# A graph attention layer in 128 rounds: how empty rows are found, who does additions and low parts, the order of scores and values, and how turned weights are loaded

## The chip, the core and the metric

One core of a Trainium2 chip. The metric is the time of one execution on the device in microseconds, as the median of several runs.

## The reference

x is (128 graphs, 128 nodes, 512), adj is (128, 128, 128). Per graph, with 16 heads of 32:

```python
q, k, v = heads(x @ Wq.T), heads(x @ Wk.T), heads(x @ Wv.T)
a = einsum('bhnd,bhmd->bhnm', q, k) * D ** -0.5 + (adj + adj)[:, None]
a = where(any(a != 0, axis=-1, keepdims=True), a, -inf)   # a row of zeros only is empty
p = nan_to_zero(softmax(a))
o = merge(einsum('bhnm,bhmd->bhnd', p, v)) @ Wo.T
return layernorm(x + o)                                   # eps 1e-5, no scale or shift
```

## The kernel before, in words

Four graphs form a group, and four heads a tile, so there are 32 groups of 4 rounds ("phases", PHASES = 128): round f treats group f // 4 and heads 4 (f % 4) to 4 (f % 4) + 3 of its four graphs. Each engine has an order of work written out by hand, and semaphores join the orders.

Precision: the weight products take operands split in a high part (rounded to FP32R) and a low part (the rest), and each product is 12 matmuls of 512 columns: low times high, high times low, high times high, over four chunks of the inner dimension. `xt_hi`, `w_hi` and `o_hi` come from ACT copies, the low parts from subtractions. A product fills one of three PSUM banks in turn (`ps_w`, `wait_bank`), and PLAN lists what is made in a round: k and q for the next round, one v for a group ahead, one output product o for the group behind.

A round f, in the orders of the engines:

- **TensorE** (L581 to L595): values of round f - 2 (`values`, L539), scores of round f (`scores`, L525), then the products of PLAN. The values need the turned softmax weights `e_t`.
- **DVE** (L884 to L901): the addition of x and an output product (`add`, L785), the bias and row maximum of the scores (`bias`, 16 instructions, L822), mean and variance of the added row (`moments`), the low part of the values (`values_lo`), and then for each half of the graphs: `any_nonzero`, `reciprocals`, `normalise` (L860) and `turn_blocks`, a transpose in blocks of 32 x 32 into `e_b` (L870).
- **POOL** (L446 to L452): the low part of a chunk of x, then `zeros` (L349) for both halves, which writes for each score whether it is zero and folds the bytes three times, and nine small instructions of LayerNorm (`ln`).
- **ACT** (L727 to L743): the high part of the values, the high part of a chunk of x, 16 exponentials with their sums (L690), with the copies of k and q after the second and fourth graph, the last step of LayerNorm (`normalise`, L667, for the row added in the round before), the v copy.
- **SP** (L308 to L325) issues all DMAs of the steady state: `save_blocks` for the second half of round f - 1 (512 KB of `e_b` to the HBM tensor `blocks`), a store of a finished row, a load of x for a later addition, a chunk of x transposed (xt), at t = 0 the adjacency of the next group, `move_blocks(f - 1)`, which is four loads of 256 KB from `blocks` to `e_t`, and `save_blocks` for the first half of round f.

The transposition of the softmax weights is done in two steps: DVE turns the blocks of 32 x 32, and the way through HBM puts the blocks in their places. `e_t` and each half of `e_b` exist once, `blocks` twice. So the loads of round f - 1 wait for both saves and for the values of round f - 2, and a transpose of DVE waits for the save of its half of the round before. Before the change each of the four loads fills 32 partitions:

```python
for b in range(BLOCKS):
    rows = slice(BLOCK * b, BLOCK * (b + 1))
    sp.dma_start(e_t[rows, :].rearrange("p (a c) -> p a c", a=BLOCKS),
                 blocks_d[f % 2, :, b].rearrange("(a j) m c -> j a (m c)", a=BLOCKS)
                 ).then_inc(moved, 16)
```

`blocks` has the shape [2, 128, 4, 2, 256] of 4 bytes, so a piece (m c) is 2 KB without a gap; a save writes pieces of 1 KB.

Of the kernel before, what the change touches and what calls it, by code (L numbers as in the profile page):

```python
# [7 lines left out]
U8 = mybir.dt.uint8  # L8
I32 = mybir.dt.int32
# [45 lines left out]
LAST = PHASES - 1  # L55
AFTER = [("o", 0, -1), ("o", 1, -1), ("o", 2, -1), ("o", 3, -1)]
# [31 lines left out]
def o_slot(g, tile):  # L88
    return tile + TILES * (g % PAIR)
# [22 lines left out]
def build(nc, xt_d, x_d, adj_d, wq_d, wk_d, wv_d, wo_d, out_d, blocks_d):  # L112
    ctx = ExitStack()
    with ctx:
# [23 lines left out]
        o_hi = sb("o_hi", [P, PAIR * TILES, 512], F32R)  # L138
        o_lo = sb("o_lo", [P, PAIR * TILES, 512], F32R)
# [4 lines left out]
        is_zero = sb("is_zero", [P, 2 * TH * NODES // 4], I32)  # L144
        folded_once = sb("folded_once", [P, 2 * TH, 16], I32)
        folded_twice = sb("folded_twice", [P, 2 * TH, 8], I32)
        folded = sb("folded", [P, 2, 2 * TH, 4], I32)
        all_zero = sb("all_zero", [P, 2, 2 * TH])
# [48 lines left out]
        zero_step = sem("zero_step")  # L197
        folded_done = sem("folded_done")
        min_done = sem("min_done")
        exp_done = sem("exp_done")  # L200
# [9 lines left out]
        normalised = sem("normalised")  # L210
        o_hi_done = sem("o_hi_done")
# [30 lines left out]
        def _(sp):  # L242
# [83 lines left out]
            for n in range(LAST - O_LAG - 1, GRAPHS):  # L326
                store(n)
# [4 lines left out]
        def _(pool):  # L332
# [16 lines left out]
            def zeros(f, half):  # L349


                n = 2 * f + half
                rows = neg_a[:, 2 * half:2 * half + 2].rearrange("p i h n -> p (i h n)")
                pool.wait_ge(biased, GG * f + 2 * half + 2)
                if n:
                    pool.wait_ge(folded_done, n)
                pool.tensor_scalar(is_zero[:, :].bitcast(U8), rows, 0.0, None, ALU.is_equal).then_inc(zero_step, 1)  # L357
                words = is_zero[:, :].rearrange("p (r c) -> p r c", r=2 * TH)
                pool.wait_ge(zero_step, 3 * n + 1)
                pool.tensor_tensor(folded_once[:, :, :], words[:, :, 0:16], words[:, :, 16:32], ALU.add).then_inc(zero_step, 1)  # L360
                pool.wait_ge(zero_step, 3 * n + 2)
                pool.tensor_tensor(folded_twice[:, :, :], folded_once[:, :, 0:8], folded_once[:, :, 8:16],  # L362
                                   ALU.add).then_inc(zero_step, 1)
                if f:
                    pool.wait_ge(min_done, n - 1)
                pool.wait_ge(zero_step, 3 * n + 3)
                pool.tensor_tensor(folded[:, half], folded_twice[:, :, 0:4], folded_twice[:, :, 4:8],  # L367
                                   ALU.add).then_inc(folded_done, 1)

            def chunk_lo(chunk):  # L370
                if chunk:
                    g, c = chunk
                    pool.wait_ge(xt_hi_done, CH * g + c + 1)
                    rest(xt_lo[:, g % PAIR, c, :], xt_raw[:, c % 2, :], xt_hi[:, g % PAIR, c, :]).then_inc(xt_lo_done, 1)

# [82 lines left out]
        def _(pe):  # L458
# [18 lines left out]
            def wait_bank(u):  # L477

                if u >= BANKS:
                    kind, g, index = USES[u - BANKS]  # L480
                    free = {"k": k_copied, "q": q_copied, "v": v_copied, "o": added}[kind]
                    pe.wait_ge(free, count(kind, g, index))
# [56 lines left out]
            def values(f, quads, out):  # L539
# [3 lines left out]
                if f:  # L543
                    pe.wait_ge(o_lo_done, f)
# [51 lines left out]

            values(LAST - 2, range(GG), ps_o)
            scores(LAST)
# [15 lines left out]
            pe.wait_ge(o_lo_done, LAST)  # L614
# [7 lines left out]
            pe.wait_ge(o_lo_done, PHASES)  # L622
# [3 lines left out]
            pe.wait_ge(o_lo_done, PHASES + 1)  # L626
# [4 lines left out]
        def _(act):  # L631
# [3 lines left out]
            def take(f, s):  # L635

                todo = slots(f)
                if not -len(todo) <= s < len(todo) or todo[s][0] == "o":
                    return
                kind, g, index = todo[s]  # L640
                in_ = ps_w[USE[kind, g, index] % BANKS][:, :]
                act.wait_ge(made[kind], count(kind, g, index))
                if kind == "v":
# [56 lines left out]
            def values_hi(f):  # L700
                g, t = f // TILES, f % TILES
                if g > 1:
                    act.wait_ge(made["o"], GG * (g - 1))
                act.wait_ge(values_done, f + 1)
                copy(o_hi[:, o_slot(g, t), :], ps_o[:, :]).then_inc(o_hi_done, 1)

            def values_hi_half(half):
                cols = slice(2 * P * half, 2 * P * (half + 1))
                bank = last_values_bank(half)
                act.wait_ge(made["o"], GG * (GROUPS - 2))  # L710
# [16 lines left out]
            for f in range(PHASES):  # L727
                if f > 1:
                    values_hi(f - 2)
# [3 lines left out]
                for i in range(GG):  # L733
                    exps(f, i)
                    if i % 2:
                        take(f, i // 2)
                if f == 0:
                    weight_hi("o")
                else:
                    normalise(f - 1, -1)  # L740
                chunk_hi(late_chunk(f))
                for s in range(2, len(slots(f))):
                    take(f, s)  # L743

            values_hi(LAST - 1)
# [12 lines left out]
        def _(dve):  # L758
# [13 lines left out]
            def values_lo(f):  # L772
                g, t = f // TILES, f % TILES
                slot = o_slot(g, t)
                dve.wait_ge(o_hi_done, f + 1)
                rest(o_lo[:, slot, :], ps_o[:, :], o_hi[:, slot, :]).then_inc(o_lo_done, 1)

            def values_lo_half(half):
# [4 lines left out]
                rest(o_lo[:, slot, cols], bank[:, cols], o_hi[:, slot, cols]).then_inc(o_lo_done, 1)  # L783

            def add(f, s):  # L785
# [12 lines left out]
                dve.tensor_tensor(row, product_bank(kind, g, i)[:, :], row, ALU.add).then_inc(added, 1)  # L798

            def moments(f, s):  # L800
# [5 lines left out]
                dve.wait_ge(added, n)  # L806
# [3 lines left out]
                dve.wait_ge(stats_done, n)  # L810
                dve.bn_aggr((last_mean_var if g == GROUPS - 1 else mean_var)[:, i, :], ln_stats[:, i % 2]).then_inc(mean_done, 1)

            def bias(f):
# [3 lines left out]
                if f:  # L817
                    dve.wait_ge(exp_done, GG * f)
                    dve.wait_ge(folded_done, 2 * f)
# [8 lines left out]
            def any_nonzero(f, half):  # L828

                n = 2 * f + half  # L830
                two = slice(2 * half, 2 * half + 2)
                if n:
                    dve.wait_ge(nonzero_done, n)
                dve.wait_ge(folded_done, n + 1)
                dve.tensor_reduce(all_zero[:, half], folded[:, half].bitcast(U8), AX.X, ALU.add).then_inc(min_done, 1)  # L835
                if f:
                    dve.wait_ge(r_done, n - 1)
                dve.wait_ge(min_done, n + 1)
                dve.tensor_scalar(nonzero[:, two].rearrange("p i h -> p (i h)"), all_zero[:, half], float(NODES), None,
                                  ALU.not_equal).then_inc(nonzero_done, 1)  # L840
# [9 lines left out]
            def normalise(f, half):  # L850
# [5 lines left out]
                dve.wait_ge(nonzero_done, n + 1)  # L856
                dve.scalar_tensor_tensor(out=r_inv[:, two], in0=recip[:, two], scalar=0.0, in1=nonzero[:, two],  # L857
                                         op0=ALU.max, op1=ALU.mult).then_inc(r_done, 1)
                dve.wait_ge(r_done, n + 1)
# [24 lines left out]
            for f in range(PHASES):  # L884
                if f:
                    add(f - 1, -1)
                bias(f)
                if f:
                    moments(f - 1, -1)
                if f > 1:  # L890
                    values_lo(f - 2)
                if f % TILES == TILES - 1 and f < LAST:
                    double_adj(f // TILES + 1)
                for half in range(2):
                    any_nonzero(f, half)
                    reciprocals(f, half)
                    normalise(f, half)
                    if f < LAST:
                        turn_blocks(f, half)
                    else:  # L900
                        add(LAST, half)  # L901
# [3 lines left out]
            moments(LAST, 0)  # L905
            values_lo_half(1)
            moments(LAST, 1)
            for half in range(2):
                for i in (2 * half, 2 * half + 1):
                    add(PHASES, i)  # L910
                    moments(PHASES, i)
# [33 lines left out]
```

## Time and profile before

| | us |
|---|---|
| timed runs | 2044.13 (2043.81 to 2044.32, three runs) |
| profiled execution | 2047.55 |
| its span | 2045.7 |
| PE, DVE, POOL, ACT busy | 1801.1, 1605.2, 1509.2, 1228.8 |
| DMA moved | 382.63 MB, 187 GB/s |
| mean granted TensorE clock | 0.942 of full speed |

PE, DVE, ACT, POOL and SP are the engines TensorE, VectorE, ScalarE, GpSimd and SyncE. "Busy" is the time in which an instruction runs; matmul records overlap, as the next begins before the last has drained, so their sum is more than the time they take. A chain of waits follows the work back from the end: at each step to what released it. The 128 rounds are alike but for the first two and the last.

### The profile page before, as it was taken

To read this page: it belongs to the slowest core of one execution; us is meant where nothing else is said; L and a number is where in the kernel's file an instruction comes from. 1 tells how busy PE (TensorE), PEld (TensorE's weight loads), DVE (VectorE), ACT (ScalarE), POOL (GpSimd) and SP (SyncE) were. 2 spreads that over 40 slices of the span, in tenths; PEclk is the share of its full clock that TensorE was granted. 3 is DMA by queue.
4 is the path that set the end of the run, shared out by engine and by line. 5 is a ranking of instruction groups with operands and counts; after the bars stand their busy time and mean duration, and the time that the engine had idled before them with its cause. 6 is when DMAs were issued, how large, how long until landed. Compare 5 with 4: busy or idle time off the path is not lost.

```text
span 2045.7 us, 46740 instructions
## 1 busy us (share of the span) xinstructions
PE 1801.1 (88%) x14370; PEld 1452.7 (71%) x14370; DVE 1605.2 (78%) x6191; ACT 1228.8 (60%) x4886; POOL 1509.2 (74%) x2292
## 2 busy tenths in 40 slices
PE   7798988989888999889889889898898989898886
PEld 5676777777776777767767777676776777777764
DVE  4887878878777878878878788787777887887786
ACT  5566566656655665566566656665665566556554
POOL 4567777777777777777777777777777777777765
PEclk9998998989999999999999899899998999999999
DMA  4667767777776677677767767777777777767664
GB/s 163 177 181 198 190 181 197 187 186 197 186 192 187 182 195 190 188 200 187 188 189 197 190 187 188 195 187 183 190 187 195 186 193 192 188 185 206 174 174 144
DMA packets 269290, 382.63 MB, mean 187 GB/s; under 512 B 19056, under 2 KB 149104, under 8 KB 268912
## 3 DMA queue, kind: packets, MB, share of 16 engines
q1 hardware_dynamic: 268464, 378.61, 69.5%
q8 instruction: 113, 1.85, 0.4%
q14 instruction: 137, 1.12, 0.2%
q10 hardware_dynamic: 576, 1.05, 0.1%
HBM read 212.86 MB, written 166.72 MB: 186 GB/s over the span
## 4 chain that ended last, share of the span: by engine, by line
POOL 43%; DMA 19%; DVE 15%; issue 10%; PE 7%; SPq 3%; ACT 1%; DVEq 0%; POOLq 0%; ACTq 0%
POOL is_zero L357 24%; DMA e_t<-blocks 15%; DVE neg_a L822 6%; POOL folded_once L360 4%; POOL xt_lo L347 4%; DVE e_sb L860 4%; DMA blocks<-e_b 3%; PE ps_s L535 3%; PE ps_o L553 3%; POOL folded_twice L362 3%; SPq L292 2%; POOL folded L367 2%; POOL ln_tmp L398 2%; DVE e_b L870 2%; DVE x_sb L798 1%
## 5 line engine op out<-in xcount | busy, mean ns | idle before, releaser
L690 ACT ACTIVATE e_sb<-neg_a,neg_max 128x128 f32<-128x128 f32 x2048 | 792.4, 392 | 71.3 <-DVE neg_max L822 70.9
L357 POOL TENSOR_SCALAR is_zero<-neg_a 128x1024 uint8<-128x1024 f32 x256 | 711.0, 2777 | 158.6 <-DVE neg_max L822 137.5
L676 ACT ACTIVATE x_sb<-x_sb,shift,rstd 128x512 f32<-128x512 f32 x124 | 100.9, 815 | 708.0 <-POOL shift L406 703.8
L822 DVE CUSTOM_DVE_ANT_0 neg_a<-ps_s,adj_sb 128x128 f32<-128x128 f32 x2048 | 441.7, 285 | 76.3 <-PE ps_s L535 76.3
L471 PE MATMUL ps_w<-xt_hi,w_lo 128*128 128x512 f32 x1020 | 426.6, 418 | 0.0
L472 PE MATMUL ps_w<-xt_lo,w_hi 128*128 128x512 f32 x1020 | 407.2, 399 | 0.0
L690 ACT ACTIVATION_READ_ACCUMULATOR e_sb<-neg_a,neg_max 128x1 f32 x2048 | 391.5, 191 | 0.0
L553 PE MATMUL ps_o<-e_t,v_sb 128*32 128x128 f32 x4080 | 167.3, 314 | 214.1 <-DMA e_t<-blocks 214.1
L870 DVE STREAM_TRANSPOSE e_b<-e_sb 128x1024 f32<-128x1024 f32 x254 | 316.3, 1245 | 27.0 <-DVE e_sb L860 0.5
L860 DVE SCALAR_TENSOR_TENSOR e_sb<-e_sb,r_inv 128x1024 f32<-128x1024 f32 x256 | 313.7, 1225 | 9.1 <-DVE r_inv L857 0.4
L553 PEld LDWEIGHTS ps_o<-e_t,v_sb 128*32 128x32 f32 x4080 | 128.0, 124 | 262.8 <-issue 261.2
L347 POOL TENSOR_TENSOR xt_lo<-xt_raw,xt_hi 128x512 fp32r<-128x512 f32 x120 | 154.9, 1291 | 201.4 <-ACT xt_hi L633 201.4
L474 PE MATMUL ps_w<-xt_hi,w_hi 128*128 128x512 f32 x1020 | 273.5, 390 | 0.0
L835 DVE TENSOR_REDUCE all_zero<-folded 128x8 f32<-128x128 uint8 x256 | 73.2, 286 | 250.3 <-POOL folded L367 250.3
L471 PEld LDWEIGHTS ps_w<-xt_hi,w_lo 128*128 128x128 f32 x1020 | 199.5, 196 | 60.8 <-issue 8.3
L472 PEld LDWEIGHTS ps_w<-xt_lo,w_hi 128*128 128x128 f32 x1020 | 199.2, 195 | 38.1
L474 PEld LDWEIGHTS ps_w<-xt_hi,w_hi 128*128 128x128 f32 x1020 | 191.5, 188 | 41.4
L471 PE MATMUL ps_w<-w_hi,xt_lo 128*128 128x512 f32 x512 | 200.3, 391 | 9.8 <-ACT k_sb L633 9.8
L472 PE MATMUL ps_w<-w_lo,xt_hi 128*128 128x512 f32 x512 | 200.1, 391 | 0.0
L471 PE MATMUL ps_w<-w_hi,o_lo 128*128 128x512 f32 x496 | 193.2, 389 | 1.1 <-DVE o_lo L760 1.1
L472 PE MATMUL ps_w<-w_lo,o_hi 128*128 128x512 f32 x496 | 193.0, 389 | 0.0
L535 PE MATMUL ps_s<-k_sb,q_sb 32*128 32x128 f32 x4096 | 188.7, 333 | 0.0
(103 smaller groups left out, 2793.7 us busy)
## 6 DMA issues: line engine op xcount, KB each, us to landing
blocks<-e_b SPq DMA_DIRECT2D x254, 512.0 KB, 3.3
e_t<-blocks SPq DMA_DIRECT2D x508, 256.0 KB, 6.3
x_sb<-x SPq DMA_DIRECT2D x124, 256.0 KB, 5.3
out<-x_sb SPq DMA_DIRECT2D x124, 256.0 KB, 4.3
xt_raw<-xt SPq DMA_DIRECT2D x120, 256.0 KB, 5.3
adj_sb<-adj SPq DMA_DIRECT2D x32, 256.0 KB, 6.4
v_sb<-wk ACTq DMA_DIRECT2D x4, 256.0 KB, 6.7
neg_a<-xt SPq DMA_DIRECT2D x4, 256.0 KB, 6.0
```

The lines of the kernel that those rows point to most:

```text
L347: return pool.tensor_tensor(out, whole, hi.bitcast(F32), ALU.subtract)
L357: pool.tensor_scalar(is_zero[:, :].bitcast(U8), rows, 0.0, None, ALU.is_equal).then_inc(zero_step, 1)
L471: pe.matmul(out, lhs_lo(c), rhs_hi(c), start=(c == 0), stop=False)
L472: pe.matmul(out, lhs_hi(c), rhs_lo(c), start=False, stop=False)
L474: last = pe.matmul(out, lhs_hi(c), rhs_hi(c), start=False, stop=(c == chunks - 1))
L535: last = pe.matmul(ps_s[h][:, nodes], q_sb[rows, slot, nodes], k_sb[rows, slot, nodes], start=True, stop=True)
L553: last = pe.matmul(out[HD * h:HD * (h + 1), i * P:(i + 1) * P], v_sb[:, g % PAIR, i, cols], weights, start=True, stop=True)
L676: act.activation(row, row, ACT.Identity, scale=rstd[:, i:i + 1], bias=shift[:, i:i + 1]).then_inc(normed, 1)
L690: last = act.activation(e_sb[:, i, h, :], neg_a[:, i, h, :], ACT.Exp, scale=-1.0, bias=neg_max[:, i, h:h + 1], accum_out=sums[:, i, h:h + 1])
L822: last = dve.tensor_tensor_reduce(out=neg_a[:, i, h, :], in0=ps_s[h][:, i * NODES:(i + 1) * NODES], in1=adj_sb[:, g % PAIR, i, :], scale=- ...
L860: dve.scalar_tensor_tensor(out=e_sb[:, two].rearrange("p i h n -> p (i h) n"), in0=e_sb[:, two].rearrange("p i h n -> p (i h) n"), scalar=BIG,
L870: dve.transpose(blocks[:, half], e_sb[:, 2 * half:2 * half + 2].rearrange("p i h (b j) -> p (i h) b j", b=BLOCKS)).then_inc(transposed, 1)
```

## The change

- `zeros` on POOL is gone. DVE finds the smallest score of a row with one reduce over all 16 rows of each partition (`smallest`), takes the larger of it and the negated other extreme (`largest`) and compares it with zero (`any_nonzero`), once a round.
- The residual addition: ACT copies the output product from PSUM to `y_sb`, POOL adds `y_sb` and x (`add`). DVE does it for the last outputs only (those counted above LATE_O).
- The low part of the values: ACT writes `o_hi` and a second full copy `o_sb`, POOL subtracts. DVE does it for the last two rounds only.
- TensorE makes the scores of a round first and then the values of two rounds before.
- ACT's high part of the values comes after the first graph's exponentials; the last step of LayerNorm, its store and the load of x come a round later.
- DVE's small instructions stand between the long ones in another order.
- The four loads of `e_t` fill 128 partitions each, a quarter of the columns.
- `o_hi` and `o_lo` have one place less: the last tile of a group has a single one.

```diff
@@ move_blocks
-                for b in range(BLOCKS):
-                    rows = slice(BLOCK * b, BLOCK * (b + 1))
-                    sp.dma_start(e_t[rows, :].rearrange("p (a c) -> p a c", a=BLOCKS),
-                                 blocks_d[f % 2, :, b].rearrange("(a j) m c -> j a (m c)", a=BLOCKS)
+                width = GG * TH * NODES // BLOCKS
+                for a in range(BLOCKS):
+                    rows = slice(BLOCK * a, BLOCK * (a + 1))
+                    sp.dma_start(e_t[:, width * a:width * (a + 1)], blocks_d[f % 2, rows].rearrange("j b m c -> b j (m c)")
                                  ).then_inc(moved, 16)
@@ SP, a round
-                store(f - O_LAG - 2)
-                load_x(f - GG)
+                store(f - O_LAG - 3)
+                load_x(f - O_LAG)
@@ POOL
+            def add(f, s):
...
+                    pool.wait_ge(x_loaded[i], 16 * (g + 1))
+                    pool.wait_ge(o_copied, count("o", g, i))
+                    pool.tensor_tensor(row, y_sb[:, :], row, ALU.add).then_inc(added, 1)
+
+            def values_lo(f):
+                pool.wait_ge(values_copied, f + 1)
+                rest(o_lo[:, o_slot(f // TILES, f % TILES), :], o_sb[:, :], o_hi[:, o_slot(f // TILES, f % TILES), :]
+                     ).then_inc(o_lo_done, 1)
...
             for f in range(PHASES):
+                if f:
+                    add(f - 1, -1)
                 chunk_lo(window_chunk(f))
-                zeros(f, 0)
-                zeros(f, 1)
+                if f > 1:
+                    values_lo(f - 2)
@@ TensorE
             for f in range(LAST):
+                scores(f)
                 if f > 1:
                     values(f - 2, range(GG), ps_o)
-                scores(f)
@@ ACT
+                if kind == "o":
+                    if g or index:
+                        act.wait_ge(added, count(kind, g, index) - 1)
+                    copy(y_sb[:, :], in_).then_inc(o_copied, 1)
...
                 copy(o_hi[:, o_slot(g, t), :], ps_o[:, :]).then_inc(o_hi_done, 1)
+                if f < LAST - 1:
+                    if f:
+                        act.wait_ge(o_lo_done, f)
+                    act.wait_ge(o_hi_done, f + 1)
+                    copy(o_sb[:, :], ps_o[:, :]).then_inc(values_copied, 1)
...
             for f in range(PHASES):
-                if f > 1:
-                    values_hi(f - 2)
+                if f and slots(f - 1)[-1][0] == "o":
+                    take(f - 1, -1)
...
                     if i % 2:
                         take(f, i // 2)
+                    elif i == 0 and f > 1:
+                        values_hi(f - 2)
...
-                    normalise(f - 1, -1)
+                    normalise(f - 2, -1)
@@ DVE
+            def smallest(f):
+                dve.wait_ge(biased, GG * (f + 1))
+                dve.tensor_reduce(neg_min[:, :].rearrange("p a b -> p (a b)"),
+                                  neg_a[:, :].rearrange("p a b c -> p (a b) c"), AX.X, ALU.max).then_inc(min_done, 1)
...
             for f in range(PHASES):
-                if f:
-                    add(f - 1, -1)
                 bias(f)
-                if f:
-                    moments(f - 1, -1)
-                if f > 1:
-                    values_lo(f - 2)
+                smallest(f)
+                reciprocals(f, 0)
+                largest(f)
+                if f:
+                    stats(f - 1, -1)
+                any_nonzero(f)
+                if f:
+                    means(f - 1, -1)
+                row_factors(f, 0)
                 if f % TILES == TILES - 1 and f < LAST:
                     double_adj(f // TILES + 1)
-                for half in range(2):
-                    any_nonzero(f, half)
-                    reciprocals(f, half)
-                    normalise(f, half)
-                    if f < LAST:
-                        turn_blocks(f, half)
-                    else:
-                        add(LAST, half)
+                normalise(f, 0)
+                if f < LAST:
+                    turn_blocks(f, 0)
+                else:
+                    add(LAST, 0)
+                reciprocals(f, 1)
+                row_factors(f, 1)
+                normalise(f, 1)
+                if f < LAST:
+                    turn_blocks(f, 1)
```

## Rows read from the trace of the kernel before

**Rows 1.** The page: busy time of each engine, share of the span, instructions.
```profile
...
PE 1801.1 (88%) x14370; PEld 1452.7 (71%) x14370; DVE 1605.2 (78%) x6191; ACT 1228.8 (60%) x4886; POOL 1509.2 (74%) x2292
```

**Rows 2.** Timeline of TensorE (start us, us, what): scores of rounds 2, 127.
```profile
...
57.40 0.39 PE L535 MATMUL ps_s<-k_sb,q_sb 32*128 32x128 f32 x4
...
2006.02 0.73 PE L535 MATMUL ps_s<-k_sb,q_sb 32*128 32x128 f32 x16
```

**Rows 3.** Chain that ended last, 1040 to 1064 us: start us, us, what.
```profile
...
1040.98 2.06 PE ps_s L535 x32
...
1044.93 2.79 POOL is_zero L357
...
1049.21 2.78 POOL is_zero L357
...
1053.42 0.30 DVE all_zero L835
...
1054.45 1.24 DVE e_sb L860
...
1055.78 1.26 DVE e_b L870
...
1057.05 4.51 DMA blocks<-e_b
...
1062.93 7.43 DMA e_t<-blocks
```

**Rows 4.** Timeline of TensorE, 1242 to 1251 us: a round's values, scores and products.
```profile
...
1242.36 1.08 PE L553 MATMUL ps_o<-e_t,v_sb 128*32 128x128 f32 x32
1243.37 1.17 PE L535 MATMUL ps_s<-k_sb,q_sb 32*128 32x128 f32 x32
1244.47 0.50 PE L471 MATMUL ps_w<-xt_hi,w_lo 128*128 128x512 f32 x1
...
1247.37 0.39 PE L471 MATMUL ps_w<-xt_hi,w_lo 128*128 128x512 f32 x1
...
1250.09 0.39 PE L471 MATMUL ps_w<-w_hi,xt_lo 128*128 128x512 f32 x1
```

**Rows 5.** Groups by line and shape, whole span: busy us, mean ns, idle before.
```profile
...
L870 DVE STREAM_TRANSPOSE e_b<-e_sb 128x1024 f32<-128x1024 f32 x254 | 316.3, 1245 | 27.0 <-DVE e_sb L860 0.5
L860 DVE SCALAR_TENSOR_TENSOR e_sb<-e_sb,r_inv 128x1024 f32<-128x1024 f32 x256 | 313.7, 1225 | 9.1 <-DVE r_inv L857 0.4
...
L347 POOL TENSOR_TENSOR xt_lo<-xt_raw,xt_hi 128x512 fp32r<-128x512 f32 x120 | 154.9, 1291 | 201.4 <-ACT xt_hi L633 201.4
...
L839 DVE TENSOR_SCALAR nonzero<-all_zero 128x8 f32<-128x8 f32 x256 | 115.3, 451 | 27.7 <-DVE all_zero L835 1.0
...
L760 DVE TENSOR_TENSOR o_lo<-ps_o,o_hi 128x512 fp32r<-128x512 f32 x127 | 83.7, 659 | 1.9 <-ACT o_hi L633 1.9
...
L798 DVE TENSOR_TENSOR x_sb<-ps_w,x_sb 128x512 f32<-128x512 f32 x124 | 80.9, 652 | 0.0
...
L633 ACT ACTIVATE q_sb<-ps_w 128x512 f32<-128x512 f32 x128 | 74.4, 581 | 0.0
...
L835 DVE TENSOR_REDUCE all_zero<-folded 128x8 f32<-128x128 uint8 x256 | 73.2, 286 | 250.3 <-POOL folded L367 250.3
```

**Rows 6.** Windows: busy us of PE, PEld, DVE, ACT, POOL; clock, DMA share, GB/s.
```profile
...
1033.00:1033.50 0.50, 0.50 (x4) 0.42 (x3) 0.41 (x3) 0.50 (x3) 0.50 (x1) 1.00 1.03 389
1058.50:1059.50 1.00, 1.00 (x6) 0.82 (x5) 1.00 (x11) 1.00 (x6) 0.12 (x1) 1.00 0.98 335
1063.50:1064.50 1.00, 1.00 (x6) 0.84 (x5) 0.80 (x2) 1.00 (x7) 0.85 (x1) 1.00 0.96 330
1065.00:1068.00 3.00, 3.00 (x14) 2.25 (x12) 2.68 (x4) 0.78 (x3) 2.69 (x6) 1.00 1.07 220
```

**Rows 7.** The page: DMA queue, and issues with KB each and median us to landing.
```profile
...
q1 hardware_dynamic: 268464, 378.61, 69.5%
...
e_t<-blocks SPq DMA_DIRECT2D x508, 256.0 KB, 6.3
```

More of the change, by code:

```diff
@@ L325, in _ @@
                     save_blocks(f, 0)
-            for n in range(LAST - O_LAG - 1, GRAPHS):
+            load_x(PHASES - O_LAG)
+            for n in range(LAST - O_LAG - 2, GRAPHS):
                 store(n)
@@ L480, in wait_bank @@
                     kind, g, index = USES[u - BANKS]
-                    free = {"k": k_copied, "q": q_copied, "v": v_copied, "o": added}[kind]
-                    pe.wait_ge(free, count(kind, g, index))
+                    free = {"k": k_copied, "q": q_copied, "v": v_copied, "o": o_copied}[kind]
+                    n = count(kind, g, index)
+                    if kind == "o" and n > LATE_O:
+                        free, n = last_added, n - LATE_O
+                    pe.wait_ge(free, n)
             def weight_product(kind, g, index, before=None, early=None):
@@ L595, in _ @@
                         weight_product(kind, g, index)
+            scores(LAST)
             values(LAST - 2, range(GG), ps_o)
-            scores(LAST)
             for _, g, index in slots(LAST):
@@ L637, in take @@
                 todo = slots(f)
-                if not -len(todo) <= s < len(todo) or todo[s][0] == "o":
+                if not -len(todo) <= s < len(todo):
                     return
                 kind, g, index = todo[s]
+                if kind == "o" and count(kind, g, index) > LATE_O:
+                    return
                 in_ = ps_w[USE[kind, g, index] % BANKS][:, :]
                 act.wait_ge(made[kind], count(kind, g, index))
-                if kind == "v":
+                if kind == "o":
+                    if g or index:
+                        act.wait_ge(added, count(kind, g, index) - 1)
+                    copy(y_sb[:, :], in_).then_inc(o_copied, 1)
+                elif kind == "v":
                     copy(v_sb[:, g % PAIR, index, :], in_).then_inc(v_copied, 1)
@@ L701, in values_hi @@
                 g, t = f // TILES, f % TILES
-                if g > 1:
+                if t == TILES - 1 and g:
+                    act.wait_ge(made["o"], GG * g)
+                elif g > 1:
                     act.wait_ge(made["o"], GG * (g - 1))
@@ L739, in _ @@
                 else:
-                    normalise(f - 1, -1)
+                    normalise(f - 2, -1)
                 chunk_hi(late_chunk(f))
                 for s in range(2, len(slots(f))):
-                    take(f, s)
+                    if slots(f)[s][0] != "o":
+                        take(f, s)
+            normalise(LAST - 1, -1)
             values_hi(LAST - 1)
@@ L809, in moments, with means @@
                 dve.bn_stats(ln_stats[:, i % 2], x_row(g, i)).then_inc(stats_done, 1)
-                dve.wait_ge(stats_done, n)
+            def means(f, s):
+                todo = slots(f)
+                if not -len(todo) <= s < len(todo) or todo[s][0] != "o":
+                    return
+                kind, g, i = todo[s]
+                dve.wait_ge(stats_done, count(kind, g, i))
                 dve.bn_aggr((last_mean_var if g == GROUPS - 1 else mean_var)[:, i, :], ln_stats[:, i % 2]).then_inc(mean_done, 1)
@@ L826, in bias, with largest, any_nonzero @@
                     last.then_inc(biased, 1)
[L828 to L835, printed above, removed]
-                if f:
[L837 to L840, printed above, removed]
+            def smallest(f):
+                dve.wait_ge(biased, GG * (f + 1))
+                dve.tensor_reduce(neg_min[:, :].rearrange("p a b -> p (a b)"),
+                                  neg_a[:, :].rearrange("p a b c -> p (a b) c"), AX.X, ALU.max).then_inc(min_done, 1)
+            def largest(f):
+                if f:
+                    dve.wait_ge(nonzero_done, f)
+                dve.wait_ge(min_done, f + 1)
+                dve.scalar_tensor_tensor(out=abs_max[:, :], in0=neg_max[:, :], scalar=-1.0, in1=neg_min[:, :],
+                                         op0=ALU.mult, op1=ALU.max).then_inc(abs_done, 1)
+            def any_nonzero(f):
+                if f:
+                    dve.wait_ge(r_done, 2 * f)
+                dve.wait_ge(abs_done, f + 1)
+                dve.tensor_scalar(nonzero[:, :], abs_max[:, :], 0.0, None, ALU.is_gt).then_inc(nonzero_done, 1)
             def reciprocals(f, half):
@@ L848, in reciprocals, with row_factors @@
                 dve.reciprocal(recip[:, two], sums[:, two]).then_inc(recip_done, 1)
-            def normalise(f, half):
+            def row_factors(f, half):
                 n = 2 * f + half
```

96 lines of the change are left out of this document (48 added, 48 removed).

## The prediction

> **What bounds the kernel now.** The busy table comes first [rows 1]: TensorE is busiest at 88%, DVE has 78%, POOL 74%. None is full, so a loop of waits must set the pace. The pace is read from the scores: those of round 2 begin at 57.40 us, those of round 127 at 2006.02 [rows 2], so 125 rounds take 1948.62, or 15.59 us each. Before them lie 57.4, behind them 2045.7 - 2006.0 = 39.7. So the span is 97.1 + 125 T, with T the length of a round. The profiled run took 2047.55 us around a span of 2045.7, and the median of the timed runs is 2044.13: the time is the span less 1.6.
>
> The chain of waits shows the loop [rows 3]: scores at 1040.98; the two zero tests on POOL from 1044.93 and 1049.21; DVE's reduce at 1053.42, normalise 1054.45, transpose 1055.78; the save to HBM from 1057.05; the four loads of e_t, which land at 1062.93 + 7.43 = 1070.36. Then TensorE does the values of that round, 1.0 us [rows 4], and only behind them the scores of two rounds later. That is 30.4 us for two rounds, 15.2 each against 15.59 measured. TensorE's own floor lies lower: values 1.01, scores 1.10, a first product of 2.90 and three of 2.72 [rows 4], together 13.2.
>
> **The zero test.** POOL loses two tests with their folds, 1053.42 - 1044.93 = 8.5 us a round [rows 3]. DVE loses two byte reduces (0.57), two nonzero instructions (0.90), the addition (0.65) and the low part of the values (0.66), together 2.8 [rows 5]. It gains one reduce over 128x2048 floats, which no row shows. By the slope between 512 elements in 0.65 and 1024 in 1.225 it takes 2.37; the bounds are 2.29 (the slope alone) and 2.61 (four times 0.65). It also gains an instruction on 16 numbers and one nonzero, 0.2 each by the nearest short row (0.29 for the byte reduce), at most 0.45. So DVE stays at 1605.2/128 = 12.5 us busy [rows 1]. Between dependent instructions 0.1 us goes (1054.45 to 1055.78 for an instruction of 1.225, rows 3 and 5), some six times a round: DVE needs 13.1. The test leaves the chain, but from now on DVE is nearly full.
>
> **ACT's copies, POOL's sums, LayerNorm.** ACT gains two evictions of 0.58 [rows 5] on 1228.8/128 = 9.6 busy [rows 1]: 10.8, hidden while a round is longer. The copies of the values are queued behind the first graph's exponentials and ahead of the other three: if the values are late, these, the q copy and DVE's first reciprocal are late too. The copy of an output product waits for POOL's addition of the round before, and TensorE's v product waits for that copy; both have most of a round. POOL gains two instructions of 1.29 [rows 5] for the 8.5 that it loses: free. LayerNorm a round later takes away a wait of ACT, an engine with 40% idle: 0. With it the loads of x and the stores come a round later in SP's queue, past one addition only, and the same number is issued: 0, and if x were late it would hold POOL, which has the room. Between nothing and 0.5 us a round for all these, on T as friction; I take 0 while another limit is far above.
>
> **Scores first.** This opens the loop. Scores no longer queue behind the values, which may come 2T + 1.2 after the scores of their own round began. They need scores 1.2, DVE 13.1, then save to landing 1070.36 - 1057.05 = 13.3 [rows 3], sum 27.6: T = 13.2. With the old loads T would be the largest of 13.2 (TensorE), 13.1 (DVE) and 13.2 (chain), and some friction where three limits meet. The stall behind the values goes; what is late next is decided by the loads.
>
> **The loads of e_t.** Before, one load writes 32 partitions and is walked with 32 outermost on both sides. Now it writes 128, in rows of 2 KB as before, but its source is walked as b, j, (m c), with b = 4 outermost. No row shows such a load; all transfers of before have 32 or 128 outermost, and the windows show a full share of all 16 engines. Prices of a packet come from the windows [rows 6], as share x 16 / packets per us: in the old e_t stage 220 GB/s is 107 packets of 2 KB, 1.07 x 16 / 107 = 159 ns; in an xt stage 0.96 x 16 / 161 = 95 ns; at best 1.03 x 16 / 190 = 87 ns; a 1 KB packet of a save takes 0.98 x 16 / 327 = 48 ns. Two outcomes are open.
>
> If a load is dealt over all 16 engines, the 512 packets of a round take 32 x 0.09 = 2.9 us and not 5.1, and the chain gains 2.2 us a round.
>
> If it is dealt out along the outermost count of both sides, it goes to 4 engines, and all four loads to the same. Each of these then has, per round, 128 packets of e_t; 64 of the saves (1024 over 16), 3.1 us; 24 of out, x and xt and 2 of adj. These 26 cost 113 ns each: the queue's 69.5% of 16 x 2045.7 is 22750 us [rows 7], less 254 x 512 x 0.048 and 508 x 128 x 0.159 leaves 6170 for 54,800 packets. So 128 x 0.09 + 3.1 + 2.9 = 17.5, and 0.3 where the queue runs dry: T = 17.8. The queue is served in order, the next saves behind this e_t and the next e_t behind those saves, so the four engines never rest, and all that the other edits save is hidden under them. The bounds are 87 ns, with T = 11.1 + 6.0 = 17.1, and 159 ns, with 20.4 + 6.0 = 26.4; from the other outcome, T = 13.3. I take four engines, since the outermost 4 is what sets these loads apart from every row, and 90 ns, since the engines here read neighbouring pieces, nearest to the xt stage.
>
> The Trainium skill (DMA: Bandwidth & Descriptors, on why a DMA increments its semaphore by 16) has a rule that speaks against the change: a transfer is split over the largest number of engines up to 16 that divides the slowest dimension of both sides, which would be 4. No trace so far holds a transfer on fewer than 16. Another page speaks for it: in SBUF — State Buffer, on the DMA port swizzle, 32 partitions reach 8 of 16 ports, some 218 GB/s. The old stage's 220 GB/s at a full share [rows 6] agrees, and by this rule alone rival A would come.
>
> **The sum.** 97.1 + 125 x 17.8 = 2322; some 10 us more at the two ends, where two or three loads lie bare and land 4 us later each (11.5 against 7.4). Less 1.6: 2330. Its own range is 2200 (T 16.8) to 2750 (T 21.1, packets near 115 ns).
>
> **Rivals.**
> A, faster: the loads use all engines. For it: the windows show them at two thirds of the xt rate with a full share, so there is something to win. Against it: the outermost 4. T is then 13.2 to 14.2; 13.6 with friction gives 97.1 + 1700 = 1797. It holds from the point where one engine's sum falls below 13: at 8 engines 5.8 + 6.0 already does.
> B, four engines in step: those that take rows j and 32 + j at one moment slow each other as in the old stage. For it: the old loads of 32 rows show 159 ns throughout. Against it: these read neighbouring pieces, and small differences pull them apart. T = 26.4, about 3400; halfway cases lie between 2750 and that.
> C, no change: T = 15.6. It needs e_t packets of 75 ns, below every row.
>
> **How the numbers follow.** The forecast has 0.50, B with the cases between 0.21, A 0.27, C 0.02. About 0.2% is what a measurement of this kernel can tell from no change. So faster 0.27, same 0.02, slower 0.71. The range goes from A's 1770 to 2750 and leaves out B.
>
> **What would show it.** From issue to landing an e_t load takes over 11 us in the forecast and under 5 in A (6.3 now, rows 7). In e_t stages the DMA share is near 0.25 with under 100 GB/s, against 1.0 and over 300. TensorE waits for e_t 4 us a round ahead of the values. DVE's reduce near 2.4 us and POOL under 55% busy show the zero test right. I am wrong if e_t lands within 6 us, or if DVE hardly idles.

## The result and the profile after

| | us |
|---|---|
| before, timed beside it | 2043.97 |
| changed kernel | 2158.68 (2157.62 to 2160.09, four runs) |
| ratio | 1.0569 (95% interval 1.0548 to 1.0591) |
| span of the profiled run | 2156.6 (before 2045.7) |

The change makes the kernel 5.7% slower. The forecast was 14% slower. The sign held, the size did not.

The page of the changed kernel, with the lines that answer to [rows 1, 7]. In the packets line, "under 512 B" counts the small writes, which are taken here for those by which DMA engines report that their share has landed.

```profile
PE 1841.4 (85%) x14370; PEld 1479.6 (69%) x14370; DVE 1596.7 (74%) x5815; ACT 1398.7 (65%) x5134; POOL 905.7 (42%) x1516
...
DMA packets 263183, 382.52 MB, mean 177 GB/s; under 512 B 12960, under 2 KB 143008, under 8 KB 262816
...
q1 hardware_dynamic: 262368, 378.59, 51.6%
...
L557 PE MATMUL ps_o<-e_t,v_sb 128*32 128x128 f32 x4080 | 178.7, 329 | 299.2 <-DMA e_t<-blocks 299.2
...
L366 POOL TENSOR_TENSOR x_sb<-y_sb,x_sb 128x512 f32<-128x512 f32 x122 | 155.0, 1270 | 415.9 <-ACT y_sb L637 415.9
...
L860 DVE TENSOR_REDUCE neg_min<-neg_a 128x16 f32<-128x2048 f32 x128 | 292.6, 2286 | 4.4
...
blocks<-e_b SPq DMA_DIRECT2D x254, 512.0 KB, 7.9
```

The lines of the page before that answer to them:

```profile
DMA packets 269290, 382.63 MB, mean 187 GB/s; under 512 B 19056, under 2 KB 149104, under 8 KB 268912
...
L553 PE MATMUL ps_o<-e_t,v_sb 128*32 128x128 f32 x4080 | 167.3, 314 | 214.1 <-DMA e_t<-blocks 214.1
...
blocks<-e_b SPq DMA_DIRECT2D x254, 512.0 KB, 3.3
```

POOL fell from 1509 to 906 us, DVE stayed (1597 against 1605), ACT rose by 170. TensorE, DVE and POOL idle more, and TensorE's wait for e_t rose from 214.1 to 299.2 us. There are 6096 fewer small writes than the 19,056 of before. That is 508 x 12, as if each of the 508 e_t loads reported from 4 engines and no longer from 16.

The scores of rounds 2 and 127 of the changed kernel, for [rows 2]:

```profile
42.63 0.84 PE L537 MATMUL ps_s<-k_sb,q_sb 32*128 32x128 f32 x20
...
2103.55 1.17 PE L537 MATMUL ps_s<-k_sb,q_sb 32*128 32x128 f32 x32
```

A round takes (2103.55 - 42.63) / 125 = 16.49 us, against 15.59. The start is 14.8 us shorter and the end 13.4 us longer, which nearly cancels, so T carries it all: 0.90 x 125 = 112 us.

Two windows in an e_t stage (same columns as [rows 6]):

```profile
1058.00:1061.00 3.00, 3.00 (x15) 2.49 (x14) 2.90 (x7) 2.89 (x14) 2.08 (x4) 1.00 0.28 104
1074.00:1077.00 3.00, 3.00 (x15) 2.47 (x14) 2.86 (x8) 2.20 (x10) 1.82 (x3) 1.00 0.25 97
```

Share 0.25 is that of 4 of 16 engines at work, at about 100 GB/s where the old loads had 220 [rows 6].

The queue of SP over one round of the changed kernel, start and duration of each issue, and the loads of the three rounds after:

```profile
1071.81 2.57 SPq L295 DMA_DIRECT2D e_t<-blocks  x4
1077.82 4.76 SPq L281 DMA_DIRECT2D blocks<-e_b  x2
1082.62 0.66 SPq L266 DMA_DIRECT2D out<-x_sb  x1
1083.32 0.80 SPq L277 DMA_DIRECT2D x_sb<-x  x1
1084.22 0.65 SPq L260 DMA_DIRECT2D xt_raw<-xt  x1
1088.75 2.62 SPq L295 DMA_DIRECT2D e_t<-blocks  x4
...
1104.78 2.50 SPq L295 DMA_DIRECT2D e_t<-blocks  x4
...
1121.69 3.00 SPq L295 DMA_DIRECT2D e_t<-blocks  x4
...
1138.17 2.28 SPq L295 DMA_DIRECT2D e_t<-blocks  x4
```

The loads go out in steps of 16.0 to 16.9 us. Both saves and the three other transfers are issued by 1085, but the next loads only go out at 1088.75. In between TensorE gets its e_t, at 1086.68:

```profile
1086.68 1.94 PE L557 MATMUL ps_o<-e_t,v_sb 128*32 128x128 f32 x32 [2.64 <-DMA e_t<-blocks]
```

So of this round 14.9 us lie between the issue of the loads and the values, and 2.1 between the values and the next issue. It is the saves' landing that holds this issue. That shows in SP's own waits (us in total, times, longest), and in the chain near the end; the chain of this profile does not reach back to the middle.

```profile
SPq L289 <- DMA blocks<-e_b: 463.5, 125, 6.6
```

```profile
2105.06 10.51 DMA blocks<-e_b
...
2115.63 0.57 SPq L295
...
2117.39 11.89 DMA e_t<-blocks
```

A save of 512 KB lands after 10.5 us here (median 7.9, before 3.3), as it would when it stands behind the loads on four engines. From the issue of the loads to their landing it is 2129.28 - 2115.63 = 13.7 us.

### The profile page after: what moved, and what is told of

Read it like the earlier page. It is cut to its first block and busy times, and to the rows that moved or that the text cites. A ratio compares the mean times of both kernels' runs of the same rounds, so it can differ in the third digit from the quotient of the medians.

```text
span 2156.6 us, 45319 instructions
## 1 busy us (share of the span) xinstructions
PE 1841.4 (85%) x14370; PEld 1479.6 (69%) x14370; DVE 1596.7 (74%) x5815; ACT 1398.7 (65%) x5134; POOL 905.7 (42%) x1516
## 3 DMA queue, kind: packets, MB, share of 16 engines
q10 hardware_dynamic: 576, 1.05, 0.1%
q14 instruction: 126, 1.03, 0.1%
## 5 line engine op out<-in xcount | busy, mean ns | idle before, releaser
L470 PE MATMUL ps_w<-xt_hi,w_lo 128*128 128x512 f32 x1020 | 465.7, 457 | 0.0
L471 PE MATMUL ps_w<-xt_lo,w_hi 128*128 128x512 f32 x1020 | 443.2, 434 | 0.0
L557 PE MATMUL ps_o<-e_t,v_sb 128*32 128x128 f32 x4080 | 178.7, 329 | 299.2 <-DMA e_t<-blocks 299.2
L350 POOL TENSOR_TENSOR o_lo<-o_sb,o_hi 128x512 fp32r<-128x512 f32 x126 | 162.7, 1291 | 472.5 <-ACT o_sb L637 472.5
L366 POOL TENSOR_TENSOR x_sb<-y_sb,x_sb 128x512 f32<-128x512 f32 x122 | 155.0, 1270 | 415.9 <-ACT y_sb L637 415.9
L860 DVE TENSOR_REDUCE neg_min<-neg_a 128x16 f32<-128x2048 f32 x128 | 292.6, 2286 | 4.4
L470 PEld LDWEIGHTS ps_w<-xt_hi,w_lo 128*128 128x128 f32 x1020 | 220.5, 216 | 82.0 <-issue 35.6
L471 PEld LDWEIGHTS ps_w<-xt_lo,w_hi 128*128 128x128 f32 x1020 | 222.5, 218 | 45.1
L637 ACT ACTIVATE y_sb<-ps_w 128x512 f32<-128x512 f32 x122 | 72.8, 597 | 242.5 <-PE ps_w L473 242.5
L883 DVE RECIPROCAL recip<-sums 128x8 f32<-128x8 f32 x256 | 48.8, 191 | 234.9 <-ACT e_sb L700 234.5
L637 ACT ACTIVATE o_hi<-ps_o 128x512 fp32r<-128x512 f32 x128 | 75.4, 589 | 187.2 <-PE ps_o L557 186.7
```

What stands on the lines that cost most here:

```text
L350: return pool.tensor_tensor(out, whole, hi.bitcast(F32), ALU.subtract)
L366: pool.tensor_tensor(row, y_sb[:, :], row, ALU.add).then_inc(added, 1)
L470: pe.matmul(out, lhs_lo(c), rhs_hi(c), start=(c == 0), stop=False)
L471: pe.matmul(out, lhs_hi(c), rhs_lo(c), start=False, stop=False)
L557: last = pe.matmul(out[HD * h:HD * (h + 1), i * P:(i + 1) * P], v_sb[:, g % PAIR, i, cols], weights, start=True, stop=True)
L637: return act.activation(out, in_, ACT.Copy, scale=scale)
```

## The experiments

Each kernel was timed beside "before" on the same chip; before took 2045.5 to 2050.0 us there. The ratio has its 95% interval.

| kernel | us | ratio |
|---|---|---|
| changed, old loads | 1742.7 | 0.851 (0.848 to 0.854) |
| before, new loads | 2382.8 | 1.162 (1.158 to 1.167) |
| changed, loads on two engines | 3437.2 | 1.678 (1.671 to 1.685) |
| changed, half of the loads old | 1864.4 | 0.909 (0.905 to 0.913) |
| before, scores first | 2015.7 | 0.984 (0.981 to 0.987) |
| changed with old loads, values first | 1842.0 | 0.901 (0.897 to 0.905) |
| before, zero test on DVE | 1932.3 | 0.942 (0.938 to 0.946) |
| the last, and scores first | 1832.8 | 0.895 (0.892 to 0.899) |
| changed, no stores | 2152.8 | 1.052 (1.049 to 1.055) |
| changed, half of the saves | 2035.7 | 0.992 (0.988 to 0.996) |
| rows of 128 | 1735.1 | 0.847 (0.844 to 0.850) |
| before, LayerNorm later | 1970.8 | 0.964 (0.959 to 0.968) |
| the last, and scores first | 1932.3 | 0.944 (0.939 to 0.948) |

**Old loads in the changed kernel.** The five lines of the new loads replaced by the five of before.

> The changed kernel with one thing undone: the four loads of e_t fill 32 partitions each, as before. Theory (four engines carry the loads, and their sum of 16.1 to 16.5 us is the round): without it the round falls to the other limits, 13.2 (TensorE) to 13.8 us, so 97 + 125 T = 1750 to 1830 us; e_t is there before the values in most rounds. Rival (the new orders and the extra ACT copies cost the time, the loads only arrive late as a result): 2050 us or more.

1742.7 us, 15% below before: a little under the forecast of 1750 to 1830, and far from the rival's 2050. Its page:

```profile
PE 1708.9 (98%) x14370; PEld 1379.7 (79%) x14370; DVE 1590.8 (91%) x5815; ACT 1369.1 (79%) x5134; POOL 963.9 (55%) x1516
```

TensorE is full and DVE nearly. TensorE's wait for e_t shrank from 299.2 to 9.4 us:

```profile
PE ps_o L557 <- DMA e_t<-blocks: 9.4, 13, 1.8
```

A round is 13.25 us, by its first and last scores at 42.81 and 1699.0. So the loads alone turn a gain of 15% into a loss of 6%. A save lands in 3.8 us (median) here, against 7.9:

```profile
blocks<-e_b SPq DMA_DIRECT2D x254, 512.0 KB, 3.8
```

**New loads in the kernel before.** The same lines the other way round.

> The kernel before with one thing done: the loads of e_t in the new form. Theory: its loop of two rounds holds one set of loads, which lands about 5 us later, so 30.4 + 5 = 35.4 for two rounds, T = 17.7, and the four engines' own sum of 16.5 stands beside it: 2250 to 2400 us, worse than the changed kernel. Rival (the new form is neutral): 2044 us.

2382.8 us, as expected; the wait for e_t went from 214.1 to 474.3 us:

```profile
PE ps_o L553 <- DMA e_t<-blocks: 474.3, 117, 9.3
```

A round is 18.1 us (first and last scores at 64.28 and 2327.36), longer than the changed kernel's 16.49 with the same loads. So the other edits still save 224 us under the new loads, where they save some 300 under the old ones.

**Two engines.**

```diff
-                    sp.dma_start(e_t[:, width * a:width * (a + 1)], blocks_d[f % 2, rows].rearrange("j b m c -> b j (m c)")
-                                 ).then_inc(moved, 16)
+                    for b in range(0, BLOCKS, 2):
+                        sp.dma_start(e_t[BLOCK * b:BLOCK * (b + 2), width * a:width * (a + 1)],
+                                     blocks_d[f % 2, rows, b:b + 2].rearrange("j b m c -> b j (m c)")).then_inc(moved, 16)
...
```

> The changed kernel with each new load split in two loads of 64 partitions, so that 2 is the outermost count of the source. Theory (the outermost count is the number of engines): two engines take 256 packets of e_t a round at 0.08 us, 20.5 us, plus 5.9 for the rest: T = 26.4 to 27.5, about 3400 to 3530 us. Rival (the price lies in the bytes, the rows or the partitions written, not in the count): near 2160 us, as all other things are equal.

3437.2 us, in the expected span. The same bytes in the same rows of 2 KB, with 2 outermost, show half the share and half the rate of the changed kernel's stage:

```profile
1022.00:1030.00 8.00, 8.00 (x37) 6.57 (x35) 6.07 (x10) 5.98 (x21) 4.28 (x10) 1.00 0.13 47
1024.00:1030.00 6.00, 6.00 (x28) 4.90 (x27) 4.11 (x6) 4.20 (x14) 3.03 (x9) 1.00 0.13 51
```

A round is (3360.78 - 42.96) / 125 = 26.54 us. Going from four engines to two adds 128 packets to each and 10.05 us: 79 ns a packet, if the rest of a round is the same in both. The rates agree: 51 GB/s from two engines is 80 ns a packet of 2 KB, and so is 102 GB/s from four (changed kernel, 1075 to 1078 us). What is not e_t in a round is then 16.49 - 128 x 0.079 = 6.4 us. SP is not what limits here: its eight issues take 12.4 us of a round (1019.02 to 1031.44), but the first three only 0.54 each or less, so the later ones seem to wait for the engines.

**Half and half.** Two of four column blocks in the new form, two in the old; six loads a round.

> The changed kernel with half of the columns of e_t loaded in the new form and half in the old one (six loads a round). Theory: the four engines then take 64 x 0.08 + 16 x 0.16 + 5.9 = 13.6 us a round, next to TensorE's 13.2: 1790 to 1900 us. Rival (a round waits for the landing of a load more than for the sum of work): about halfway between the changed kernel and the run with old loads, 1950 to 2000 us.

1864.4 us, inside the forecast of the theory. It rules out the rival of 1950 to 2000. The sum of 13.6 with TensorE's 13.2 beside it is a little short: a round takes 14.1 us, and the span of 1852.5 is 6% above that of the run with old loads.

**Scores first alone.** The two calls swapped in TensorE's loop and at its end.

> The kernel before with one thing done: TensorE makes the scores of a round ahead of the values of two rounds before. Theory (the loop scores, zero test, turn, save, load, values, scores set the pace): the loop opens, and POOL's own work is next, 8.5 for the zero tests, 3.5 for LayerNorm and 1.2 for a chunk, T = 13.3 to 14.3: 1760 to 1890 us. Rival (POOL's zero test sets the pace, whatever the order): 1990 us or more.

2015.7 us: over the forecast of 1760 to 1890 and over the rival's 1990 as well. The loop through the values was not the only one. The chain of this run, on POOL:

```profile
1002.33 0.47 POOL folded_once L360
...
1006.83 0.19 POOL shift L406
1007.01 2.38 issue
...
1009.43 1.29 POOL xt_lo L347
1010.72 2.76 POOL is_zero L357
```

The 2.38 us after `shift` (LayerNorm's last value) are given to no one there. ACT's timeline fills them:

```profile
1007.05 0.82 ACT L676 ACTIVATE x_sb<-x_sb,shift,rstd 128x512 f32<-128x512 f32 x1 [6.07 <-POOL shift L406]
1007.77 0.58 ACT L633 ACTIVATE v_sb<-ps_w 128x512 f32<-128x512 f32 x1
1008.25 0.59 ACT L633 ACTIVATE o_hi<-ps_o 128x512 fp32r<-128x512 f32 x1
1008.72 0.63 ACT L633 ACTIVATE xt_hi<-xt_raw 128x512 fp32r<-128x512 f32 x1
```

ACT waits for POOL's `shift`, then does four things in order, the last of which POOL's `xt_lo` needs, and the zero tests stand behind that. It is a second chain that sets the pace in this stretch: the tests with their folds 8.3 (1010.72 to the fold that ends at 1019.06), LayerNorm 3.5, this gap 2.4, the low part 1.3, together 15.5 us a round. More than half of it are the zero tests, which the change takes off POOL.

**Values first in the changed kernel with old loads.** The two calls swapped back.

> The run with old loads (1743 us) with the values made first again. Theory: the loop is closed, scores 1.1 + DVE 13.1 + save to landing 12 to 13.3 + values 1.0 for two rounds, T = 13.6 to 14.3: 1800 to 1885 us. Rival (the order is worth nothing once the zero test is off POOL): 1743 us.

1842.0 us, as forecast: here the order is worth 5.7% (1743 against 1842).

**The zero test alone, and with scores first.** `smallest`, `largest` and `any_nonzero` of the change put into the kernel before, `zeros` taken out; then also the order of scores.

> The kernel before with one thing done: the empty rows are found on DVE (one reduce, one maximum, one comparison a round); additions and low parts stay on DVE, values first, old loads. Theory: the loop loses 8.5 of POOL and gains 2.3 of DVE, but DVE's order is now 14.5 a round and closes the loop at (1.1 + 14.5 + 13.3 + 1.0) / 2 = 15.0: 1930 to 1980 us. Rival (DVE is the bound as it stands): over 2044 us.

> As the run with the zero test on DVE, and scores first: all of the change but the additions and low parts on POOL, LayerNorm later and the new loads. Theory: DVE's own work bounds it, 14.3 to 14.7 a round: 1885 to 1935 us. Rival (TensorE bounds it, and the ACT copies are for nothing): 1745 to 1770 us.

1932.3 us, as forecast; 1832.8, below the forecast of 1885 to 1935, as DVE's order takes 13.8 us a round where I had 14.3. DVE and TensorE are both close to full there:

```profile
PE 1726.0 (95%) x14370; PEld 1391.3 (76%) x14370; DVE 1719.5 (94%) x6063; ACT 1243.7 (68%) x4886; POOL 536.5 (29%) x1268
```

The remaining step to 1743 is what the ACT copies and POOL's sums give, together with LayerNorm later and the order of DVE's small instructions; these were not told apart.

**No stores.**

```diff
                     sp.wait_ge(normed, n + 1)
-                    sp.dma_start(out_d[g, :, i, :], x_row(g, i)).then_inc(stored[i], 16)
+                    if g == GROUPS - 1:
+                        sp.dma_start(out_d[g, :, i, :], x_row(g, i)).then_inc(stored[i], 16)
...
```

This kernel leaves out the stores of 31 of the 32 groups, and its loads of x wait for the normalised row alone.

> The changed kernel without the stores of the rows but those of the last group (31 of 32 groups of the output are not written), and the next load of x waits for the normalised row only. Theory (a round is the sum of the work that the four busy engines have): 8 packets of 2 KB less on each engine a round, 0.7 to 0.9 us, so 2158 - 90 to 110: 2050 to 2070 us. Rival (a round is the latency of save, load and values, and the stores lie beside it): within 15 us of 2158.

2152.8 us against 2158.7: 6 us, where the sum of work gives 90 to 110. A round is 16.45 us. My theory of a sum over everything falls.

**Half of the saves.**

```diff
-                sp.dma_start(blocks_d[f % 2, :, :, half], blocks_half[:, half]
+                n = BLOCKS if f < 2 else BLOCKS // 2
+                sp.dma_start(blocks_d[f % 2, :, 0:n, half], blocks_half[:, half, 0:n]
...
```

This kernel leaves out half of each save from the third round on, so the loads read old data in its place.

> The changed kernel with saves of half the bytes: from the third round on only two of four blocks of each row are written, so the loads read old data for the others. It takes 32 packets of 1 KB, 1.5 us, off each engine a round, more bytes of engine time than the stores had. Theory (a round is: loads on the four engines, then the saves that stand behind them, then the time from the saves' landing to the first packet of the next loads, in which stores, x and xt are hidden): 1.5 us less a round, 2158 - 188: 1960 to 1985 us. Rival 1 (sum of all work of the four engines): the same. Rival 2 (the saves are hidden as the stores were, and the loop is loads and values alone): over 2140 us.

2035.7 us, which misses the forecast of 1960 to 1985 and lies far from rival 2's 2140: 0.94 us a round by its scores (15.55), of 1.5 taken off. Saves are on the path where stores are not. The rest seems to be taken over by the next wait, as SP's waits show: in half of the rounds (63 waits against 62) the loads now wait for the values to free e_t.

```profile
SPq L290 <- PE ps_o L558: 215.8, 63, 6.6
SPq L290 <- DMA blocks<-e_b: 144.9, 62, 7.1
```

**Rows of 128.** The tensor in HBM gets the order a, b, j, so a load is 128 rows in one run; each save becomes four DMAs of 32 partitions (not shown below).

```diff
...
-                    rows = slice(BLOCK * a, BLOCK * (a + 1))
-                    sp.dma_start(e_t[:, width * a:width * (a + 1)], blocks_d[f % 2, rows].rearrange("j b m c -> b j (m c)")
-                                 ).then_inc(moved, 16)
+                    sp.dma_start(e_t[:, width * a:width * (a + 1)],
+                                 blocks_d[f % 2, a].rearrange("b j m c -> (b j) (m c)")).then_inc(moved, 16)
...
```

> The changed kernel, but the tensor in HBM is laid out so that each load reads 128 rows of 2 KB in one run (128 outermost on both sides) and fills 128 partitions; for it each save is four DMAs of 32 partitions. Theory: with 128 outermost all 16 engines work, and 1740 to 1760 us come out, TensorE's bound; in the e_t stage the rate is 330 to 390 GB/s in place of 220. Rival (128 partitions are the trouble, not the count): over 2000 us.

1735.1 us, 5 us under the forecast. Two windows in its e_t stages:

```profile
1018.00:1019.00 1.00, 1.00 (x7) 0.81 (x6) 0.90 (x2) 1.00 (x6) 0.84 (x3) 1.00 1.07 408
1003.50:1004.50 1.00, 1.00 (x6) 0.84 (x5) 1.00 (x1) 1.00 (x7) 1.00 (x2) 1.00 1.05 393
```

Filling 128 partitions is no trouble; with 128 outermost it gives 400 GB/s, against 220 for 32 partitions [rows 6] and 100 for the new form. Both this and the run with old loads were timed again side by side:

> The run with old loads once more, beside the one with rows of 128 on the same chip, to tell the two apart: TensorE's 13.1 us a round bounds both. Expected 1740 to 1746 us. If the time were set by the e_t loads in some rounds, it would lie over the other by what its e_t stage is longer.

> The run with rows of 128 once more. Theory: both are bound by TensorE, and the loads' faster landing gives only the last rounds, where no other work covers a load: 3 to 8 us less than with old loads. Rival: the two are equal within 0.1%.

1743.7 and 1734.9 us (ratios 0.8517, 0.8498 to 0.8537, and 0.8474, 0.8456 to 0.8493). It is the fastest version here, by 8.8 us, where 3 to 8 were forecast and in the last rounds alone. Of the 6.4 us between the spans of the two profiled runs, 4 lie in the rounds (13.25 against 13.21) and 2 at the ends; TensorE's wait for e_t fell from 9.4 to 1.4 in the first pair of runs.

**LayerNorm later, alone and with scores first.** `normalise(f - 2, -1)` on ACT, store and load of x a round later, in the kernel before.

> The kernel before with one thing done: the last step of LayerNorm, its store and the load of x a round later. Theory: the loop through the values stays closed, so little: 2000 to 2048 us. Rival (a second loop, LayerNorm on POOL, ACT's last step, v copy, high part of the values, high part of the chunk, POOL's low part, zero tests, sets the pace by itself): 1850 us or less.

> The kernel before with scores first and with the last step of LayerNorm a round later. Scores first alone gave 2016 us where 1760 to 1890 were expected, and its trace shows POOL idle 2.4 to 2.9 us a round between LayerNorm and the chunk, waiting for ACT, which waits for LayerNorm. Theory (two loops of nearly the same length, one through the values, one through POOL and ACT; both must be opened): POOL's own 13.3 us a round and DVE's 13.2 are left, T = 13.5 to 14.5: 1785 to 1910 us. Rival (POOL and DVE wait for each other in the zero test, whatever ACT does): 1980 us or more.

1970.8 and 1932.3 us. LayerNorm later is worth 3.6% alone, more than scores first, and 4.1% on top of it. So in the kernel before both loops held. Neither forecast was met (2000 to 2048 and 1785 to 1910), and neither rival's time came (1850 or less, 1980 or more): the second still takes 14.7 us a round ((1932.6 - 97) / 125), and 65% of its chain is POOL, with DVE 16%:

```profile
1001.11 2.80 POOL is_zero L358
...
1005.40 2.78 POOL is_zero L358
...
1012.97 0.13 POOL xt_lo L348
1014.17 1.29 POOL xt_lo L348
1015.54 2.80 POOL is_zero L358
```

POOL's own order nearly fills that stretch: from the first zero test of one round to that of the next it is 14.4 us (1001.11 to 1015.54). With the zero test off POOL the kernel with scores first takes 1833 us.

## Why the prediction was wrong

**The mechanism was right in its main part.** The new loads go to 4 engines (6096 fewer reports, share 0.25, 104 GB/s), and they set the pace of the changed kernel: with the old loads it takes 1743 us. "All that the other edits save is hidden under them" goes too far, since the kernel before takes 2383 us with the new loads. The other edits bring a round down from 18.1 us to the 16.5 that the loop through the four engines allows; only what they would save below that is hidden. The rule of the Trainium skill on how many engines a transfer uses (DMA: Bandwidth & Descriptors, on why a DMA increments its semaphore by 16) agrees with the three counts tried, 16, 4 and 2. The Trainium skill's port map (SBUF — State Buffer, on the DMA port swizzle), which spoke for rival A, agrees too where all engines are used: 220 GB/s into 32 partitions against 400 into 128.

**The failed step is the size of "128 x 0.09".** A packet of e_t takes 79 ns, not 90, so the term is 10.1 us a round and not 11.5. The bound of 87 ns, the best row, was above it as well. The method is at fault: share x 16 / rate counts the time of packets that overlap more than once, as a share of 1.03 says. The pace is engines / rate: 16 / 190 gives 84 ns, nearer. And 90 was a choice above the best row. Over 125 rounds that is 175 us, about all of the 171 us by which I was too high; the rest of the sum was 0.1 us too low a round. The 10 us at the two ends did not come. The bare loads cost 12.5 us at the end (53.1 against 40.6 with old loads), but round 2 begins 14.8 us earlier, which the sum had left out. It begins at 45.67 with the zero test alone on DVE and at 54.49 with scores first alone (57.40 before), so most of this is the zero test's.

**The rest of the sum was right in size and wrong in kind, which is luck.** I had 3.1 for saves + 2.9 for 26 packets + 0.3 = 6.3 us; measured are 6.4. But the stores are not in it: without them a round loses 0.04 us. Halving the saves takes off 0.94. "These four engines never rest" was false: the loop is one of loads, saves and landings. In the round shown above, 14.9 us pass from the issue of the loads to the values, of which the packets of e_t are 10.1, and 2.1 from the values to the next issue, which waits for the saves to land. The other 4.8 us lie before the first packet of e_t, where the store, x and xt issued before stand ahead of it in the queue, and between its last packet and TensorE's start; how they divide was not measured.

**The other edits.** DVE busy 12.5 expected, 1596.7/128 = 12.5 measured; the reduce 2.37 expected, 2.29 measured, my lower bound. ACT 10.8, measured 10.9. The floor of 13.2 for TensorE and 13.1 for DVE: with old loads a round is 13.25, so next to nothing was lost by friction, and rival A's 13.6 was too careful; its condition, loads on all engines, failed in the changed kernel. Rival B, engines in step at 159 ns, is ruled out by the 79. TensorE waits 2.4 us a round for e_t, not 4 (299.2 us in 112 waits). I had 17.8 - 13.2 = 4.6 us between the round and TensorE's own work. The round is 16.5, and TensorE's work took 1.0 us a round more than with old loads (busy 1841.4 against 1708.9 us), at a mean granted clock of 0.924 against 0.996, so 2.3 are left.

**LayerNorm later at 0 was reasoned wrongly and stays untested.** I called ACT's wait harmless since ACT has 40% idle, and I had read the chain in one stretch only. In the kernel before, this wait closes a second loop by way of POOL, 15.5 us a round in the run of scores first, and opening it alone gives 3.6%. But 8.3 of these 15.5 us are the zero tests, which the change takes off POOL, and POOL is busy for 42% of the changed kernel. No run has the changed kernel with LayerNorm early, so whether the 0 holds there is open.

## What to carry to other kernels

Look at the outermost count of both sides of a DMA before looking at bytes and partitions: here 4 in place of 128 made the kernel 24% slower (2159 against 1735 us), and the same 128 partitions with 128 outermost were the fastest of all. An engine with idle time can still close a loop, as ACT does in the kernel before, so an edit that removes its wait is costed by following who waits for what it does next. Price a stage by its pace (engines over packets per us), and try what lies in a gap by leaving it out, since a sum of work can come out right for the wrong reason.

## What the runs showed of the hardware

- One DMA engine takes a 2 KB packet of these loads every 79 to 80 ns, whether four or two work (26 GB/s each at 102 GB/s on four and 51 on two; the windows shown have 97 to 104 and 47 to 51).
- Loads on 16 engines reach 393 to 408 GB/s into 128 partitions, and 220 into 32 partitions at the same share of 1.05 to 1.07. So the share alone does not show the loss.
- A load on few engines delays transfers that use all: a save of 512 KB lands in 7.9 us (median) beside loads on four engines and in 3.8 beside the old loads of the otherwise same kernel.
- The granted clock followed TensorE's idleness: 0.996 in the run where TensorE was 98% busy, 0.924 in the changed kernel, 0.757 with two engines at 58% busy. Full speed (2.4 GHz) is 1.00; the changed kernel was granted 0.50 (1.2 GHz) from 1070 to 1071 us, after TensorE had waited 1.81 us for e_t.
